# A decoder layer on one core: the routed-token table two steps behind its one-hot rows, gates scaled earlier, semaphores cleared on five engines

## The chip, the cores and the metric

The kernel runs on one core of one Trainium2 chip. A core has five engines that run their own instruction streams and meet only through semaphores: PE (matrix multiply), DVE (VectorE, elementwise work and reductions), ACT (ScalarE, activation functions and copies), POOL (GpSimd) and SP (SyncE, which here issues most of the DMAs). The metric is the device time of one execution, in microseconds (us); lower is better.

## The reference

The input `x` is 4 sequences of 512 tokens with 512 features, in float32. Three residual blocks follow one another, each on a layer-normalised input:

```
x = x + self_attention(layernorm(x))     # 16 heads of 32, rotary, causal, a window of 128 keys
x = x + cross_attention(layernorm(x), ctx)   # 32 heads of 16, RMS-normed q and k, softmax over 512 keys
x = x + moe(layernorm(x))                # 64 experts, 8 per token, at most 256 tokens per expert
```

The last block matters here. A router gives each token 64 logits; the softmax of its 8 largest, scaled to sum to one, are its gates. Tokens are numbered within each expert in order of appearance, those beyond 256 are dropped, and each expert runs `down(silu(gate(x)) * up(x))` on its own tokens. The results are added to the tokens' rows, weighted by the gates.

## The kernel before, in words

Three phases follow one another: `self_attention` (`sa`), `cross_attention` (`xa`) and `experts` (`ex`). Each holds its semaphores and buffers in a `Phase`, and the phases are separated by barriers of all engines. When a phase's block ends, `Phase.clear` opens a further block in which SP clears the phase's semaphores one by one (line 69), and a barrier ends that block too. This happens for six groups of semaphores: `sw` (10), `sa` (47), `xw` (8), `xa` (85), `ex` and `ew` (33 together).

The cross-attention phase is a list of steps written out by hand (`WALK`). Every engine's program is a loop over the same steps `w`, and functions such as `hot_step` or `rt_step` say in which step a piece of work stands. A batch of the attention takes 32 steps (`STEPS`), so the four batches are steps 0 to 127. In step `w`:

- PE computes the scores of step `w` (line 1420, two banks of `xa_ring`) and then the product with the values for step `w - 1` (line 1432); ACT computes the exponentials of step `w` in between (line 1038).
- Every fourth step (`w` = 1 modulo 4) PE transposes a finished group of heads (`turn_out`, line 1440). Before that DVE copies it out of the accumulator (`take_values`, line 1289, one step earlier); after it DVE divides by the sums and adds to the residual (`take_out`, lines 1205 to 1211).
- Beside this run the projections of the next batch and the routing of the batch before: `turn_route` (PE, 1378), its split into a high and a low part (ACT 1056, DVE 1199), the logits (`project_route`, PE, lines 75 to 77), `take_logits` (DVE 1217, 1219), then the choice of 8 experts, the positions, and the gates.

Engines take their instructions in the order written, so an instruction that waits holds all that stands behind it on its engine.

The routing ends in a table: for each expert and place, which token stands there. It is made for 16 tiles of 128 tokens, numbered `n`. For each tile DVE writes 8 pairs of 128x128 one-hot matrices in f16 (`slots`, lines 1269 and 1271) and PE adds their products into one PSUM bank (`add_to_table`, line 1407). The one-hot matrices have two buffers, used in turn:

```
if n >= 2:
    dve.wait_ge(s_tab, n - 1)       # slots(n): the table matmuls of tile n-2 are done
pe.wait_ge(s_hot, n + 1)            # add_to_table(n): the one-hot rows of tile n are written
```

Both sides of tile `n` stand in the step `hot_step(n)`. For the tiles of the first three batches, n = 0 to 11, these are the steps 98, 100, ... 112 and 116, 118, 120, 122, inside the attention of the last batch. The four tiles of the last batch can only come after the attention, and all stand in step 138, behind that batch's own routing.

At the end of the phase, DVE scales the last batch's gates (`scale_gates`, lines 1256 and 1258) after these four tiles, SP stores them (`store_gates`, line 916) and then issues the weight loads of expert 3 (`load_weights`, lines 1491 to 1497); those of experts 1 and 2 were issued in step 131. DVE turns the finished table into token numbers (`take_table`, lines 1277 to 1281). Then SP waits for its stores, and the barrier of the phase follows.

Of the kernel before, what the change touches and what calls it, by code (L numbers as in the profile page):

```python
# [16 lines left out]
B, S, D = 4, 512, 512  # L17
T = S // P
NT = B * T
# [23 lines left out]
class Phase:  # L43
# [20 lines left out]
    def clear(self):  # L64
        with self.nc.Block() as block:
            @block.sync
            def _(sp):
                for s in self.sems:
                    sp.sem_clear(s)


def product(pe, out, hi_l, lo_l, hi_r, lo_r, chunks, part=None, stop=True):
# [542 lines left out]
def cross_attention(nc, consts, ident, stage, shared, w_w, weights_of, context, w_router, x1, x2, xn3, token, target):  # L615
# [12 lines left out]
    with ExitStack() as ctx:  # L628
# [181 lines left out]
            return pos_step(b) + 1  # L810

        def hot_step(n):
            return STEPS * (B - 1) + 2 * (n + 1 + n // (2 * T)) if n < NT - T else pos_step(B - 1) + 1

        WALK = range(begin(0, 0) - 2, STEPS * B + 13)
        TILES = [(n, j) for n in range(B) for j in range(KQ)]
        ROUTED = [(b, t) for b in range(B) for t in range(T)]

# [69 lines left out]
        @block.sync  # L888
        def _(sp):
            def load_x(n, t):  # L890
                if n >= 2:
                    sp.wait_ge(st_x[t], 16 * (n - 1))
                    sp.wait_ge(s_xr, (n - 2) * T + t + 1)
                sp.dma_start(xs[:, n % 2, t], x1[n * T + t]).then_inc(ld_x[n % 2][t], 16)

            def load_context(n, t):
                before = (n, t - 2) if t >= 2 else (n - 1, t + 2)
                if before[0] >= 0:
                    sp.wait_ge(s_b0, USE["x", *before] + 1)
                sp.dma_start(cx[:, t % 2], context[n * T + t]).then_inc(ld_c[t], 16)  # L900

            def store_turned(n, j):
                sp.wait_ge(s_free, USE["kn", n, j] + 1)
                for part in range(2):
                    sp.dma_start(turned[n % 2, j // T, part, :, j % T * P:(j % T + 1) * P].rearrange("(c p) t -> p c t", p=P),
                                 hl[:, part].bitcast(F32)).then_inc(st_h, 16)

            def load_weights(experts):
                sp.wait_ge(s_pv, STEPS * B)
                for e in experts:  # L910
                    weights_of.load_gate_up(sp, e, e)
                    weights_of.load_down(sp, e, e)

            def store_gates(b):
                sp.wait_ge(s_gt, b + 1)
                sp.dma_start(xn3[b * T:(b + 1) * T, :, D:XW].rearrange("n p e -> p n e"), gates).then_inc(st_g, 16)

            def load_turned(n, q, side):
                sp.wait_ge(st_h, 32 * (n * KQ + T * (side + 1)))
                if n > 0:  # L920
                    for i in range(2):
                        sp.wait_ge(s_sc[i], STEPS * (n - 1) + 2 * T * (q + 1))
                rows = turned[n % 2, side].rearrange("a (pair i d) t -> a i d pair t", i=2, d=D2)
                for r, part in enumerate(((0, 1, 0), (0, 0, 1))[side]):
                    for i in range(2):
                        at_row = i * W2 + r * D2
                        sp.dma_start((kT, qT)[side][at_row:at_row + D2, 4 * q:4 * q + 4, :].bitcast(F32),
                                     rows[part, i, :, 4 * q:4 * q + 4, :]).then_inc(ld_h[q], 16)

            def store_x2(b, t):  # L930
                sp.wait_ge(s_x2, (b + 1) * G)
                sp.dma_start(x2[b * T + t], xs[:, b % 2, t]).then_inc(st_x[t], 16)

            def store_normal(b, t):
                sp.wait_ge(s_xr, b * T + t + 1)
                sp.dma_start(xn3[b * T + t, :, 0:D], xn[:, route_slot(t)]).then_inc(st_n[t], 16)

            for n in range(2):
                for t in range(T):
                    load_x(n, t)  # L940
            for w in WALK:
                for n, t in at(lambda n, t: x_step(n - 1, T - 1) + 2, w, [(n, t) for n in range(1, B) for t in range(2)]):
                    load_context(n, t)
                for n, t in at(lambda n, t: x_step(n, t - 2), w, [(n, t) for n in range(B) for t in range(2, T)]):
                    load_context(n, t)
                for n, j in at(kn_step, w, TILES):
                    store_turned(n, j)
                    if n == 0 and T <= j < KQ - 1:
                        load_turned(0, j - T, 0)
                if w == kn_step(0, KQ - 1):  # L950
                    for q in range(3):
                        load_turned(0, q, 1)
                for n in range(1, B):
                    if w == kn_step(n, T - 1) + 1:
                        load_turned(n, 0, 0)
                        load_turned(n, 1, 0)
                    if w == kn_step(n, KQ - 1):
                        for q, side in ((0, 1), (1, 1), (2, 0), (2, 1)):
                            load_turned(n, q, side)
                for n in range(B):  # L960
                    if w == STEPS * n:
                        for side in range(2):
                            load_turned(n, 3, side)
                if w > STEPS and w % STEPS == 2:
                    for t in range(T):
                        store_x2(w // STEPS - 1, t)
                if w == STEPS * B:
                    load_weights(range(1))
                for r in at(rn_step, w, ROUTED):
                    store_normal(*r)  # L970
                if w == rn_step(B - 1, T - 1):
                    load_weights(range(1, 3))
                for b in range(B):
                    if w == gate_step(b):
                        store_gates(b)
                for n, t in at(lambda n, t: rn_step(n - 2, t), w, [(n, t) for n in range(2, B) for t in range(T)]):
                    load_x(n, t)
            load_weights(range(3, weights_of.AHEAD))
            for t in range(T):
                sp.wait_ge(st_x[t], 16 * B)  # L980
                sp.wait_ge(st_n[t], 16 * B)
            sp.wait_ge(st_g, 16 * B)
# [119 lines left out]
        def _(dve):  # L1102
# [188 lines left out]
            for w in WALK:  # L1291
# [25 lines left out]
                for b in range(B):  # L1317
                    if w == sel_step(b):
                        choose(b)
                for n in range(NT):  # L1320
                    if w == hot_step(n):
                        slots(n)
                for b in range(B):
                    if w == gate_step(b):
                        scale_gates(b)
            take_table()
            dve.wait_ge(s_x2, B * G)

# [1 line left out]
        def _(pe):  # L1330
# [112 lines left out]
            for w in WALK:  # L1443
# [19 lines left out]
                    if 0 <= step < (C if j < T else 2):  # L1463
                        project(n, j, step)
                for n in range(NT):
                    if w == hot_step(n):
                        add_to_table(n)


# [393 lines left out]
```

## Time and profile before

| | us |
|---|---|
| median of 3 runs (lowest to highest) | 1760.61 (1759.91 to 1761.31) |
| the profiled execution | 1763.67 |
| its span, first to last instruction | 1761.9 |
| PE busy in it | 1443.3 (82%) |
| DVE busy, ACT busy | 1052.7, 980.6 |
| mean granted clock of PE | 0.914 of full |

The span is divided roughly so: the self-attention phase ends at 520, the exponentials of the cross-attention run from 633 to 1165, the routing of the last batch from there to 1208, and the first work of the experts begins at 1216. Busy time is the time in which an engine had an instruction in flight. "Idle before, releaser" in a row gives how long the engine had been idle and which instruction ended that. A queue row (`SPq`, `DVEq`) is an instruction of an engine's instruction stream that does no data work, such as a barrier (`DRAIN`, `EVENT_SEMAPHORE`) or a DMA issue.

### The profile page before, as it was taken

The page shows a single profiled execution, that of the slowest core. Times are in us where ns is not written, and L with a number is a line of the kernel's source. Part 1 is how long each engine was busy: PE and PEld are TensorE (multiplying, and loading weights), DVE is VectorE, ACT ScalarE, POOL GpSimd, SP SyncE. Part 2 cuts the span into 40 slices and gives each one's busy share as a digit, 9 for nine tenths or more (in the row PEclk, how much of TensorE's full clock was granted, in tenths as well). Part 3 has the DMA queues.
Part 4 walks back from the last instruction along what each step waited for, and adds up shares of the span by engine and source line. Part 5 has one row for each costly group of instructions (what it writes and reads, how often), then busy time and mean ns, then how long its engine had stood idle before and what let it go on. Part 6 is the DMA issues. An engine that isn't in the chain of part 4 may idle for free. (4 is left out here: it accounts for less than half of the span.)

```text
span 1761.9 us, 28899 instructions
## 1 busy us (share of the span) xinstructions
PE 1443.3 (82%) x9667; PEld 1066.1 (61%) x9667; DVE 1052.7 (60%) x2102; ACT 980.6 (56%) x1982; POOL 771.0 (44%) x494
## 2 busy tenths in 40 slices
PE   3988898989966578988988856672999999999990
PEld 2777776777744444444444323242899999999880
DVE  4667576666636524344444453445888888888880
ACT  3555454545532246755755733431777787777770
POOL 2444343443432024434434400001577777777762
PEclk9999899989987989999999976775999999999995
DMA  8000000000012581691681670033799999999986
GB/s 308 1 25 13 13 25 25 13 13 25 7 36 72 116 147 56 116 188 37 111 180 35 110 123 1 4 128 120 212 300 291 301 301 296 296 299 288 294 169 120
DMA packets 133108, 229.82 MB, mean 130 GB/s; under 512 B 17865, under 2 KB 51145, under 8 KB 132496
## 3 DMA queue, kind: packets, MB, share of 16 engines
q1 hardware_dynamic: 103184, 154.98, 32.3%
q0 software_dynamic: 29248, 72.53, 18.6%
q8 instruction: 63, 1.03, 0.2%
q10 hardware_dynamic: 576, 0.98, 0.2%
q14 instruction: 37, 0.30, 0.1%
HBM read 163.78 MB, written 71.83 MB: 134 GB/s over the span
## 5 line engine op out<-in xcount | busy, mean ns | idle before, releaser
L1038 ACT ACTIVATE shared<-xa_ring 128x1024 f32<-128x1024 f32 x256 | 247.2, 1029 | 142.9 <-PE xa_ring L1420 142.6
L1000 POOL TENSOR_TENSOR shared<-shared,xa_half 128x32 f32<-128x32 f32 x24 | 130.3, 5429 | 244.7 <-DVE shared L1159 244.7
L282 POOL TENSOR_TENSOR sa_prob<-sa_prob,sa_rinv 128x1024 f32<-128x1024 f32 x64 | 121.3, 1896 | 247.5 <-DVE sa_rinv L445 247.5
L1587 POOL DMA_INDIRECT ex_xg<-xn,token x128 | 169.3, 1322 | 86.5 <-issue 56.8
L340 ACT ACTIVATE sa_prob<-sa_sc_ps,sa_nmax 128x256 f32<-128x256 f32 x256 | 118.0, 473 | 113.4 <-DVE sa_nmax L432 113.4
L75 PE MATMUL ex_ba<-ex_xh,ex_wh 128*128 128x256 f32 x512 | 150.8, 295 | 5.8 <-DVE ex_xl L1701 3.7
L1432 PE MATMUL xa_out<-shared 128*17 128x512 f32 x1024 | 148.4, 654 | 0.6 <-ACT shared L1038 0.4
L76 PE MATMUL ex_ba<-ex_xl,ex_wh 128*128 128x256 f32 x512 | 146.1, 285 | 0.0
L77 PE MATMUL ex_ba<-ex_xh,ex_wl 128*128 128x256 f32 x512 | 146.0, 285 | 0.0
L1688 DVE TENSOR_TENSOR ex_wl<-shared,ex_wh 128x1024 fp32r<-128x1024 f32 (+1 forms) x128 | 116.9, 955 | 41.0 <-ACT ex_wh L1631 40.9
L432 DVE TENSOR_REDUCE sa_nmax<-sa_sc_ps 128x2 f32<-128x512 f32 x128 | 83.1, 687 | 67.6 <-PE sa_sc_ps L577 67.6
L1420 PE MATMUL xa_ring<-xa_qT,xa_kT 64*128 64x512 f32 x512 | 107.0, 489 | 12.6 <-DMA xa_qT<-turned 6.3
L1598 POOL DMA_INDIRECT out_dram<-ex_y,target x64 | 104.5, 1632 | 23.1 <-issue 23.1
L1631 ACT ACTIVATE ex_wh<-shared 128x1024 fp32r<-128x1024 f32 (+1 forms) x128 | 100.2, 832 | 25.4 <-PEq L1538 25.4
L1598 POOL DMA_INDIRECT odd_sum<-ex_y,target x64 | 104.3, 1629 | 22.5 <-issue 19.2
L75 PEld LDWEIGHTS ex_ba<-ex_xh,ex_wh 128*128 128x128 f32 x512 | 98.9, 193 | 22.4 <-issue 22.4
L76 PEld LDWEIGHTS ex_ba<-ex_xl,ex_wh 128*128 128x128 f32 x512 | 99.3, 194 | 0.0
L77 PEld LDWEIGHTS ex_ba<-ex_xh,ex_wl 128*128 128x128 f32 x512 | 99.3, 194 | 0.0
L573 PE MATMUL sa_sc_ps<-sa_mask,sa_identb 128*128 128x512 bf16 x128 | 53.7, 419 | 43.8 <-DVE sa_kT L412 30.9
L1701 DVE TENSOR_TENSOR ex_xl<-ex_bx,ex_xh 128x512 fp32r<-128x512 f32 x128 | 82.6, 686 | 9.5 <-issue 7.0
L1420 PEld LDWEIGHTS xa_ring<-xa_qT,xa_kT 64*128 64x128 f32 x512 | 43.5, 201 | 70.5 <-issue 37.7
L75 PE MATMUL sa_pr_ps<-sa_wh,sa_xh 128*128 128x512 f32 x192 | 84.6, 441 | 1.5 <-DVE sa_xl L389 1.5
(235 smaller groups left out, 4024.4 us busy)
## 6 DMA issues: line engine op xcount, KB each, us to landing
shared<-in_L_ffn_gate_proj_dram SPq DMA_DIRECT2D x64, 384.0 KB
shared<-in_L_ffn_up_proj_dram SPq DMA_DIRECT2D x64, 384.0 KB
turned<-stage SPq DMA_DIRECT2D x64, 256.0 KB, 2.8
shared<-in_L_ffn_down_proj_dram SPq DMA_DIRECT2D x64, 256.0 KB
xa_kT<-turned SPq DMA_DIRECT2D x96, 128.0 KB, 7.3
xa_qT<-turned SPq DMA_DIRECT2D x96, 128.0 KB, 9.0
shared<-in_L_ffn_down_proj_dram SPq DMA_DIRECT2D x64, 128.0 KB
sa_x<-in_x_dram SPq DMA_DIRECT2D x16, 256.0 KB, 2.8
```

What stands on the lines that cost most here:

```text
L75: pe.matmul(out, hi_l(c), hi_r(c), start=(c == 0), stop=False)
L76: pe.matmul(out, hi_l(c), lo_r(c), start=False, stop=False)
L77: last = pe.matmul(out, lo_l(c), hi_r(c), start=False, stop=(stop and c == chunks - 1))
L282: pool.tensor_tensor(prob[:, 4 * g:4 * g + 4, :], prob[:, 4 * g:4 * g + 4, :], rinv[:, 4 * g:4 * g + 4].unsqueeze(2).to_broadcast([P, 4, 2 ...
L340: act.activation(prob[:, h, :], sc_ps[p][:, i, :], ACT.Exp, bias=nmax[:, h:h + 1], accum_out=rsum[:, h:h + 1]).then_inc(s_ex[p], 1)
L1000: pool.tensor_tensor(power[:, i], ms[:, i], half[:], ALU.pow).then_inc(s_pw, 1)
L1038: act.activation(prob[:, w % 2, 2 * i:2 * i + 2, :], ring[i][:], ACT.Exp, scale=D2 ** -0.5).then_inc(s_ex[i], 1)
L1420: last = pe.matmul(ring[u][:, i, :], kT[half, pair, kt * P:(kt + 1) * P], qT[half, pair, :], start=True, stop=True)
L1432: last = pe.matmul(out_ps[32 * i:32 * i + D2 + 1, :], v[:, b % 2, kt, 4 * g + i, :], prob[:, w % 2, i, :], start=(kt == 0), stop=(kt == T ...
L1587: pool.indirect_dma_start(out=xg[:, e % RING, j, :], out_offset=None, in_=xn3, in_offset=bass.IndirectOffsetOnAxis(token[:, at:at + 1], 0))\
L1598: pool.indirect_dma_start(out=odd_sum if e % 2 else out, out_offset=bass.IndirectOffsetOnAxis(target[:, at:at + 1], 0), in_=y[:, e % RING, ...
L1688: dve.tensor_tensor(lo, src, hi.bitcast(F32), ALU.subtract).then_inc(s_wl, 1)
```

## The change

Four edits are made. The table matmuls of tile `n` stand two steps behind its one-hot rows on PE; the last four tiles' rows are spread over steps 138 and 139, so their matmuls stand in steps 140 and 141, and `WALK` is a step longer. In a step, `scale_gates` stands ahead of `slots`. The loads of expert 3's weights stand with those of experts 1 and 2 in step 131, ahead of the last gates' store. Each semaphore group is cleared on all five engines, a fifth on each.

```diff
@@ class Phase, def clear
             @block.sync
             def _(sp):
-                for s in self.sems:
+                for s in self.sems[0::5]:
                     sp.sem_clear(s)
+
+            @block.tensor
+            def _(pe):
+                for s in self.sems[1::5]:
+                    pe.sem_clear(s)
...
(the same on vector [2::5], scalar [3::5] and gpsimd [4::5])
@@ cross_attention
         def hot_step(n):
-            return STEPS * (B - 1) + 2 * (n + 1 + n // (2 * T)) if n < NT - T else pos_step(B - 1) + 1
+            return STEPS * (B - 1) + 2 * (n + 1 + n // (2 * T)) if n < NT - T else pos_step(B - 1) + 1 + n % T // 2
-        WALK = range(begin(0, 0) - 2, STEPS * B + 13)
+        WALK = range(begin(0, 0) - 2, STEPS * B + 14)
@@ SP
                 if w == rn_step(B - 1, T - 1):
-                    load_weights(range(1, 3))
+                    load_weights(range(1, weights_of.AHEAD))
...
-            load_weights(range(3, weights_of.AHEAD))
             for t in range(T):
                 sp.wait_ge(st_x[t], 16 * B)
@@ DVE
+                for b in range(B):
+                    if w == gate_step(b):
+                        scale_gates(b)
                 for n in range(NT):
                     if w == hot_step(n):
                         slots(n)
-                for b in range(B):
-                    if w == gate_step(b):
-                        scale_gates(b)
@@ PE
                 for n in range(NT):
-                    if w == hot_step(n):
+                    if w == hot_step(n) + 2:
                         add_to_table(n)
```

## Rows read from the trace of the kernel before

**Rows 1.** The page: busy us, share of the span and instructions of each engine.
```profile
PE 1443.3 (82%) x9667; PEld 1066.1 (61%) x9667; DVE 1052.7 (60%) x2102; ACT 980.6 (56%) x1982; POOL 771.0 (44%) x494
```

**Rows 2.** Waits from 1017 to 1156: who waited for whom, us, times, longest.
```profile
ACT shared L1038 <- PE xa_ring L1420: 80.6, 23, 6.7
...
PE xa_pr L1407 <- DVE stage L1271: 49.4, 12, 5.7
```

**Rows 3.** Timeline, steps 99 to 101: start us, us, engine, line, operation [idle before].
```profile
1026.07 1.94 ACT L1038 ACTIVATE shared<-xa_ring 128x1024 f32<-128x1024 f32 x2 [6.70 <-PE xa_ring L1420]
...
1029.06 1.94 ACT L1038 ACTIVATE shared<-xa_ring 128x1024 f32<-128x1024 f32 x2 [1.05 <-PE xa_ring L1420]
...
1030.45 0.66 PE L1378 MATMUL xa_b<-ident,xa_xn 128*128 128x128 f32 x4
...
1033.03 1.38 DVE L1269 TENSOR_SCALAR stage<-xa_from,xa_row 128x128 f16<-128x128 f16 x8
1034.33 1.86 DVE L1271 TENSOR_SCALAR stage<-xa_from,xa_column,xa_token 128x128 f16<-128x128 f16 x8
...
1036.25 1.04 PE L1407 MATMUL xa_pr<-stage 128*128 128x128 f16 x8 [5.14 <-DVE stage L1271]
...
1038.05 1.94 ACT L1038 ACTIVATE shared<-xa_ring 128x1024 f32<-128x1024 f32 x2 [6.31 <-PE xa_ring L1420]
```

**Rows 4.** Timeline: the exponentials of steps 98, 123 with 124, and 126 with 127.
```profile
1017.43 1.94 ACT L1038 ACTIVATE shared<-xa_ring 128x1024 f32<-128x1024 f32 x2 [1.08 <-PE xa_ring L1420]
...
1155.02 3.77 ACT L1038 ACTIVATE shared<-xa_ring 128x1024 f32<-128x1024 f32 x4 [3.03 <-PE xa_ring L1420]
...
1161.51 3.77 ACT L1038 ACTIVATE shared<-xa_ring 128x1024 f32<-128x1024 f32 x4 [0.61 <-PE xa_ring L1420]
```

**Rows 5.** Windows: us, busy of PE, PEld, DVE, ACT, POOL, PEclk, DMA share, GB/s.
```profile
1017.43:1161.51 144.08, 90.93 (x531) 36.59 (x529) 63.66 (x268) 58.30 (x73) 2.60 (x6) 0.75 0.19 35
896.00:1016.00 120.00, 102.37 (x599) 50.33 (x599) 48.26 (x116) 71.76 (x101) 47.87 (x20) 0.93 0.51 103
1155.02:1163.40 8.38, 7.64 (x52) 2.20 (x50) 1.80 (x4) 7.60 (x9) 0.00 (x0) 1.00 0.01 2
1190.00:1206.00 16.00, 4.01 (x29) 2.83 (x29) 14.78 (x75) 1.04 (x7) 0.00 (x0) 0.50 0.01 2
```

**Rows 6.** Timeline: normalising for routing; a logits product at full clock; table matmuls; the gates' exponentials.
```profile
1024.13 0.73 DVE L1140 TENSOR_SCALAR xa_xn<-stage,xa_mv,xa_rstd 128x512 f32<-128x512 f32 x1
...
1051.77 0.30 PE L75 MATMUL xa_b<-xa_rh,xa_route_h 128*128 128x64 f32 x1
...
1053.34 0.23 DVE L1217 COPY xa_logits<-xa_b 128x64 f32<-128x64 f32 x1 [0.73 <-PE xa_b L77]
...
1117.26 0.30 ACT L1075 ACTIVATE xa_ex<-xa_top,xa_negative 128x8 f32<-128x8 f32 x1
...
1119.35 3.74 ACT L1038 ACTIVATE shared<-xa_ring 128x1024 f32<-128x1024 f32 x4
...
1136.76 0.62 PE L1407 MATMUL xa_pr<-stage 128*128 128x128 f16 x8 [2.71 <-DVE stage L1271]
```

**Rows 7.** Timeline of the phase's end: scaling of the gates, the last weight load's issue.
```profile
1206.11 0.43 DVE L1258 TENSOR_TENSOR xa_xn<-xa_xn,xa_total 128x256 f32<-128x256 f32 x1
...
1208.49 0.47 SPq L1497 DMA_DIRECT2D shared<-in_L_ffn_down_proj_dram  x1
```

**Rows 8.** Line 628, the phase's barrier: ns min/median/max, first and last start us.
```profile
L628 DVEq DRAIN  x1: 17/17/17, 1208.2 to 1208.2; - x1
...
L628 SPq DRAIN  x1: 7/7/7, 1209.5 to 1209.5; - x1
```

**Rows 9.** Line 69, the clears: the whole span, then 1209 to 1216 alone.
```profile
L69 SPq EVENT_SEMAPHORE_RANGE_CLEAR  x183: 25/30/49, 23.6 to 1761.6; - x183
...
L69 SPq EVENT_SEMAPHORE_RANGE_CLEAR  x85: 25/30/49, 1209.7 to 1215.0; - x85
```

**Rows 10.** Line 65, the clearing block's barrier: the semaphore instruction of PE.
```profile
L65 PEldq EVENT_SEMAPHORE  x1: 51/51/51, 1215.2 to 1215.2; - x1
```

More of the change, by code:

```diff
@@ L67, in _ @@
             def _(sp):
-                for s in self.sems:
+                for s in self.sems[0::5]:
                     sp.sem_clear(s)
+            @block.tensor
+            def _(pe):
+                for s in self.sems[1::5]:
+                    pe.sem_clear(s)
+            @block.vector
+            def _(dve):
+                for s in self.sems[2::5]:
+                    dve.sem_clear(s)
+            @block.scalar
+            def _(act):
+                for s in self.sems[3::5]:
+                    act.sem_clear(s)
+            @block.gpsimd
+            def _(pool):
+                for s in self.sems[4::5]:
+                    pool.sem_clear(s)
 def product(pe, out, hi_l, lo_l, hi_r, lo_r, chunks, part=None, stop=True):
```

## The prediction, made before the changed kernel was run

> **What bounds the kernel now.** I read the page first: PE is busy for 82% of the span [rows 1], so the other 18% are where to look. The experts' part is back to back PE work that no edit touches; the change bears on the last batch of the cross-attention (from step 98), on the phase's end, and on the blocks that clear semaphores. So next I took the waits of the last batch. PE waited 12 times, 49.4 us in all, for the last one-hot row of a tile, and ACT, which does nothing late by itself, waited 80.6 us for PE's scores [rows 2]. The timeline of steps 99 to 101 shows how: PE ends its own work of step 100 with a transpose at 1030.45 + 0.66 us; DVE only starts the tile's one-hot rows at 1033.03 and ends at 1036.2; PE's table matmuls start at 1036.25 after 5.14 us of idleness, and the next exponentials come at 1038.05, 9.0 us after the last ones. The step before, without a table, took 3.0 us [rows 3]. So DVE's 3.2 us (1.38 + 1.86) and all that DVE does ahead of them stand on the path once every other step. The windows show what this costs in clock: the stretch ran at a mean granted clock of 0.75 while DVE was busy 63.7 of 144.1 us and ACT 58.3; undisturbed steps at its end ran at 1.00 with PE busy 7.64 of 8.38 us [rows 5].
>
> **The table matmuls.** Nothing is added or removed, 96 matmuls go two steps down PE's list. I take the stretch from the exponentials of step 98 (1017.43) to those of step 126 (1161.51): 28 steps, seven groups of four, 144.1 us [rows 4, 5]. What would it take without the 12 waits?
> - Attention alone at full clock: steps 123 to 125 take 6.49 us and step 126 half of 3.77, so 8.4 a group, 58.7 for seven [rows 4].
> - 12 tables at 0.62 (the full-clock price), 7.4; four logits products at 1.57 (1051.77 to 1053.34), 6.3 [rows 6]; four transposes at 0.66, 2.6 [rows 3], and after three of the products about 0.4 each until DVE has copied the logits (0.23 plus the hand-over, an estimate), 1.2 [rows 6].
> - The positions' few matmuls, an estimate of 1.0 from the table's price; the gates on ACT, 2.1 (1117.26 to 1119.35) [rows 6]; four high-part copies on ACT, which fills 7.60 of 8.38 us by itself [rows 5]: at half an exponential (0.5) each, of which 1.3 shows.
> - A wait that appears: the first routed tile is normalised on DVE behind tile 0's one-hot rows and is ready at 1024.13 + 0.73 = 1024.9 [rows 6]; PE now comes for it at about 1017.4 + 2 x 2.1 + 0.9 = 1022.5. 2.4 us.
>
> The sum is 83.0, a gain of 61 at full clock. At the clock mix of the other batches' routing (0.93, [rows 5]), 14% of 83 us are at half clock, where a plain step takes 3.0 us instead of 1.9 [rows 3, 4]; that gives back 4.6. What else may be late: `slots(n)` now stands ahead of `take_out` of the next step, whose bank PE wants two steps later. DVE needs 3.25 + 0.7 us for both, PE takes 0.6 (table) + 2.5 + 1.9 until then, a cover of 1 us; where a routed tile's low part comes first (steps 104, 106, 110) the cover is about gone. Over seven groups DVE has 9.1 us of work in 11.9. I take off 2.5 us for that. The buffers are no new wait: `slots(n)` needs the table of tile n-2, which stands at least two steps earlier on PE. Value taken: **54 us**. Lower end 47 (the 49.4 of waits less the 2.4 that appear, and no clock back), upper end 61. It is far nearer to the upper working than to a half of it, since each term has a row.
>
> The Trainium skill ("TensorE: Matmul & The Clock Gate", Part 1) says that the array's half rate is its default and that activity releases it. By that rule alone, PE without idle waits stays at full clock and the sum is the 61 us; the trace agrees as far as it goes, with clock 0.75 where PE idled 49 us and 1.00 in the undisturbed group [rows 2, 5].
>
> **Rows of the last four tiles and the gates.** Steps 138 to 141 hold nothing else on PE, so two steps of distance change nothing there; PE still waits for DVE's last tile. DVE is the bound: 14.78 of 16 us busy [rows 5]. Scaling the gates first puts its 0.43 us [rows 7] and a small reciprocal, with the hand-over some 0.6, on that path: DVE reaches the barrier at 1208.2 + 0.6 = 1208.8 instead of 1208.2 [rows 8]. SP had been last, at 1209.5 [rows 8], since it stored the gates after the last row and then issued four weight loads up to 1208.96 [rows 7]. Both are now done four tiles (13 us) earlier. So the phase ends with DVE: 0.65 us gained, between 0 and 1. The four loads come earlier on SP, in a place where SP next waits for the gates anyway; the gates' store queues behind one more expert's weights, but the DMA engines were idle at 0.01 from 1190 to 1206 [rows 5], so it has ten us to spare. Cost nothing; if that cover were gone, the barrier would wait for it, some us. The experts' first weights were in time before and are not later now.
>
> **The clears.** SP's 85 clears run from 1209.7 to 1215.0, 63 ns each though an instruction takes 30; there are 183 [rows 9]. All stand between two barriers with every other engine idle, hence on the path: 183 x 0.06 = 11.1 us. By groups of 10, 47, 8, 85, 25 and 8, the longest share of one engine is 2 + 10 + 2 + 17 + 5 + 2 = 38 clears, 2.4 us at SP's pace. Gain **8.7**. The trace shows no clear on another engine. From one side, they cost as on SP or a bit less: 9.0. From the other, PE's barrier instruction takes 51 ns [rows 10] against the clear's 30, so 90 ns a clear: 3.4 us, gain 7.7; I put the low end at 7.
>
> **Sum.** 54 + 8.7 + 0.65 = 63.3. Against the profiled execution (span 1761.9 and 1.8 around it, 1763.7) that is 1700.4; the median of the runs is 3.1 lower, so **1697.3**.
>
> **The rivals.**
> - Clock all back: PE is fed so steadily that the 4.6 and the 2.5 us aren't lost. 61 + 9.3 = 70.4, so 1690. For it: the undisturbed steps. Against: the 2.4 us stall, and the batches before, with less idleness than now, were at 0.93. Chance 0.17.
> - Clock not back: the stretch keeps its mix, PE having small gaps in every step. 47 + 9.3 = 56.3, so 1704. Chance 0.18.
> - DVE becomes the bound: it takes over the order, and each of the 12 one-hot groups makes PE wait for the `take_out` or the low part behind it, about 1.1 us each (the length of `take_out`), 13 us from the 56: gain 43 + 9.3, so 1708. For it: the thin cover above. Against: 77% of DVE's time. Chance 0.1.
> - The change doesn't do what it says: the 49 us were hidden beside something else (a load of keys, ACT), and the stretch stays: only the 9.3 us come, 1751. Against: ACT waits 80.6 us for PE and for nothing else there [rows 2]. Chance 0.02.
> - Slower: the clears. Instructions of a kind that only SP has run so far, in new program parts on four engines, are slow to fetch or to run on one of them. Place: the six clearing blocks; it decides from (63.3 + 2.4) / 38 = 1.7 us a clear, against 63 ns now. At 2 us each: 38 x 2 = 76 us against a gain of 54.7 + 11.1, so 1771. Against: PE's 51 ns [rows 10]. Chance 0.02.
>
> **How the numbers follow.** The forecast has 0.51, at 1697, by itself 1693 to 1702. To hold 8 of 10 the range takes in half-way to each neighbour and both clock cases: 1688 to 1709. A change within 0.2% (3.5 us) is what a measurement here can't tell from none. Faster by more: forecast and the first four rivals, 0.97; slower 0.02; within it 0.01.
>
> **What would show it.** Right: in the stretch no wait of PE's table matmuls for DVE longer than a few tenths of a us; 28 steps in 83 to 97 us; clock there 0.9 or more; a first wait of PE for the normalised tile of 1 to 3 us; the clears of the big group within 1.1 to 1.6 us; the phase's last barrier set by DVE. Wrong: PE waiting at the logits or transposes for DVE's `take_out` or copies (DVE the bound), clock below 0.85 with no waits (the second rival), or a clear pitch above 0.1 us on any engine. Should the stretch shrink as worked out and the total not, something in the experts has moved, for which I have no row.

## The result and the profile after

The changed kernel takes 1686.6 us (median of 4 runs, 1675.9 to 1692.4) against 1760.3 before (4 runs, 1757.4 to 1761.3): a ratio of 0.958 [0.953, 0.963]. The forecast was 1697, with a range of 1688 to 1709; the kernel is 1.4 us faster than the range's lower end. The profiled executions took 1692.4 and 1763.7 us, 71.3 us apart where 63.3 were forecast.

The page of the changed kernel answers to [rows 1]: PE does the same 9667 matmuls and is busy for 84% of a shorter span. The second line is from the page's list of costliest groups: ACT waits 76.4 us for scores in the whole kernel; the same line of the kernel before had 142.6.

```profile
PE 1424.7 (84%) x9667; PEld 1062.2 (63%) x9667; DVE 1050.2 (62%) x2102; ACT 978.9 (58%) x1982; POOL 772.4 (46%) x494
...
L1057 ACT ACTIVATE shared<-xa_ring 128x1024 f32<-128x1024 f32 x256 | 247.1, 1030 | 76.5 <-PE xa_ring L1439 76.4
```

The waits of PE for other engines in the changed kernel, from the exponentials of step 98 to those of step 126, answer to [rows 2]. Columns: us in total, times, longest.

```profile
PE xa_ring L1439 <- ACT shared L1057: 2.7, 6, 1.0
PE xa_b L1397 <- DVE xa_xn L1159: 2.2, 1, 2.2
PE xa_b L1397 <- DVE xa_logits L1236: 1.2, 3, 0.4
PE xa_b L95 <- DVE xa_scaled L1226: 0.8, 1, 0.8
...
PEld xa_pr L1426 <- DVE stage L1290: 6.0, 7, 0.9
```

The wait of the table matmuls for the one-hot rows, 49.4 us in 12 pieces, is gone. What is left was foreseen: one wait of 2.2 us for the normalised tile, three of 0.4 for the logits, and one of 0.8 for `take_out`. The last line is of the weight loads (`PEld`), which run beside the matmuls: for 7 of the 12 tables they still waited for a row, up to 0.9 us, while PE was busy with its own work of the step. So the rows are ready in time, but not by much.

The windows of the changed kernel answer to [rows 5]: the same 28 steps, a stretch of the batch before, and the phase's end up to the clears. Columns as in [rows 5].

```profile
1017.41:1096.67 79.26, 72.25 (x531) 30.58 (x529) 62.89 (x268) 58.08 (x73) 2.60 (x6) 0.94 0.32 61
896.00:1016.00 120.00, 101.52 (x599) 49.96 (x599) 48.08 (x116) 71.37 (x101) 47.85 (x20) 0.93 0.47 100
1096.67:1144.00 47.33, 23.68 (x135) 18.46 (x133) 29.64 (x120) 8.36 (x20) 1.22 (x2) 0.58 0.44 147
```

The stretch starts within 0.02 us of where it did and takes 79.3 us instead of 144.1: 64.8 less, out of the 71.3. The same 531 matmuls now fill 72.25 us instead of 90.93, because the granted clock in the stretch is 0.94 where it was 0.75. That is near the 0.93 of the stretch ahead of it, which the change doesn't touch.

The timeline around step 100 answers to [rows 3]. Columns: start us, us, engine, line, operation [idle before].

```profile
1026.71 1.94 ACT L1057 ACTIVATE shared<-xa_ring 128x1024 f32<-128x1024 f32 x2 [0.53 <-PE xa_ring L1439]
...
1027.48 1.39 DVE L1288 TENSOR_SCALAR stage<-xa_from,xa_row 128x128 f16<-128x128 f16 x8
...
1028.78 1.87 DVE L1290 TENSOR_SCALAR stage<-xa_from,xa_column,xa_token 128x128 f16<-128x128 f16 x8
...
1030.25 1.94 ACT L1057 ACTIVATE shared<-xa_ring 128x1024 f32<-128x1024 f32 x2 [1.60 <-PE xa_ring L1439]
...
1031.35 0.62 PE L1426 MATMUL xa_pr<-stage 128*128 128x128 f16 x8
...
1032.44 1.94 ACT L1057 ACTIVATE shared<-xa_ring 128x1024 f32<-128x1024 f32 x2 [0.25 <-PE xa_ring L1439]
```

DVE's one-hot rows take as long as before (1.39 + 1.87), but they end at 1030.6, and the table matmuls that stand in the list at 1031.35 find them ready; the next exponentials come 2.2 us after the last ones.

The clears answer to [rows 9]. The first line is SP's share of the group of 85 at the end of the cross-attention, the others PE's and DVE's, from the instructions of the lines that hold them in the changed kernel. Columns: ns min/median/max, first and last start us.

```profile
L69 SPq EVENT_SEMAPHORE_RANGE_CLEAR  x17: 25/25/35, 1144.0 to 1145.0; - x17
...
L74 PEldq EVENT_SEMAPHORE_RANGE_CLEAR  x17: 56/56/56, 1144.1 to 1146.0; - x17
...
L79 DVEq EVENT_SEMAPHORE_RANGE_CLEAR  x17: 54/54/54, 1144.1 to 1145.4; - x17
```

SP starts a clear every 57 ns, DVE every 83, PE every 117 (ACT 67 and POOL 64 by the same reading). PE's 17 clears last 1.9 us and set the block's end. In the line below, the phase's last barrier, DVE is the last to come (PE's drain started 2 us earlier), as in the forecast.

```profile
L648 DVEq DRAIN  x1: 17/17/17, 1143.8 to 1143.8; - x1
```

Where the 71.3 us come from: 64.8 from the stretch; 0.85 from the rest of the phase (48.18 to 47.33); 3.2 between the big group's first clear and the experts' first instruction (6.70 to 3.51); 0.8 behind the experts (2.34 to 1.50); 1.6 from the experts' part (543.15 to 541.53), which no edit touches. At step 98 the two executions are level, though the clearing blocks before it are 1.5 us shorter in the changed one; the same code around them took that much longer there.

### The profile page after: what moved, and what is told of

The parts are those of the page before. It is cut to its first block and busy times, and to the rows that moved or that the text cites. A ratio compares the mean times of both kernels' runs of the same rounds, so it can differ in the third digit from the quotient of the medians.

```text
span 1690.5 us, 28899 instructions
## 1 busy us (share of the span) xinstructions
PE 1424.7 (84%) x9667; PEld 1062.2 (63%) x9667; DVE 1050.2 (62%) x2102; ACT 978.9 (58%) x1982; POOL 772.4 (46%) x494
## 5 line engine op out<-in xcount | busy, mean ns | idle before, releaser
L1057 ACT ACTIVATE shared<-xa_ring 128x1024 f32<-128x1024 f32 x256 | 247.1, 1030 | 76.5 <-PE xa_ring L1439 76.4
L1606 POOL DMA_INDIRECT ex_xg<-xn,token x128 | 173.3, 1354 | 83.0 <-issue 60.5
L97 PE MATMUL ex_ba<-ex_xh,ex_wl 128*128 128x256 f32 x512 | 146.1, 285 | 0.0
L1451 PE MATMUL xa_out<-shared 128*17 128x512 f32 x1024 | 140.5, 622 | 0.5 <-ACT shared L1057 0.4
L1439 PE MATMUL xa_ring<-xa_qT,xa_kT 64*128 64x512 f32 x512 | 103.4, 473 | 14.0 <-DMA xa_qT<-turned 7.5
L1665 ACT ACTIVATE ex_sg<-ex_ba 128x256 f32<-128x256 f32 x64 | 24.5, 383 | 108.6 <-PE ex_bb L97 108.6
```

The costliest lines, as they stand in the source:

```text
L97: last = pe.matmul(out, lo_l(c), hi_r(c), start=False, stop=(stop and c == chunks - 1))
L1057: act.activation(prob[:, w % 2, 2 * i:2 * i + 2, :], ring[i][:], ACT.Exp, scale=D2 ** -0.5).then_inc(s_ex[i], 1)
L1439: last = pe.matmul(ring[u][:, i, :], kT[half, pair, kt * P:(kt + 1) * P], qT[half, pair, :], start=True, stop=True)
L1451: last = pe.matmul(out_ps[32 * i:32 * i + D2 + 1, :], v[:, b % 2, kt, 4 * g + i, :], prob[:, w % 2, i, :], start=(kt == 0), stop=(kt == T ...
L1606: pool.indirect_dma_start(out=xg[:, e % RING, j, :], out_offset=None, in_=xn3, in_offset=bass.IndirectOffsetOnAxis(token[:, at:at + 1], 0))\
```

## Experiments

All runs give "stretch" from the exponentials of step 98 to those of step 126, and "tail" from there to the first clear. Totals of single executions scatter by some 5 us, since the self-attention ended at any time from 507.9 to 520.6 us with the same code; so parts are compared by these stretches, and totals by the ratios of runs on one chip.

**1. Each part alone, and the changed kernel again.**

```
table_only    + hot_step of the last four tiles: + n % T // 2; WALK one longer
              - if w == hot_step(n):          (add_to_table on PE)
              + if w == hot_step(n) + 2:
clears_only   - for s in self.sems: sp.sem_clear(s)
              + for s in self.sems[i::5]: engine_i.sem_clear(s)   on five engines
tail_only     + scale_gates ahead of slots; load_weights(range(1, AHEAD)) in step 131
```

> The changed kernel once more, beside its three parts. Both theories: 1675 to 1692 as its four runs had it, median near 1687; stretch from the exponentials of step 98 to those of step 126 79 to 85 us in its profile.

> Only the table matmuls two steps behind their one-hot rows (with the spread of the last four tiles). Theory A (nearly all of the extra 10 us over the forecast lies in this stretch: the table matmuls hide half beside the exponentials, and neither the clock nor DVE takes back what was set aside for them): 65 us faster than before, about 1695, stretch 79 to 81 us. Rival B (the forecast's 54 us was right for this part and the rest came from the end of the phase and the experts' start): 54 us faster, about 1706.

> Only the clears on five engines. From PE's pace of 117 ns a clear in the changed kernel's trace, 38 clears in sequence cost 4.4 us: theory A 6 us faster than before (5 to 7), 1754. Rival B (clears and what they start earlier give 8.7 or more): 1751 or less.

> Only the gates' scaling ahead of the last rows and expert 3's weights loaded with those of experts 1 and 2. Theory A: the phase's barrier 0.6 to 0.9 us earlier, total within 1 us of that, 1759.5. Rival B (the earlier weight loads free the DMA engines for the experts' first gathers): 2.5 us or more faster.

Against the kernel before on the same chip (1758.75, 23 runs): the changed kernel 0.9575 [0.9541, 0.9610]; the tables alone 0.9624 [0.9586, 0.9661], so 66 us; the clears alone 0.9963 [0.9941, 0.9985], 6.5 us; the tail's edits 0.9988 [0.9967, 1.0009], 2.1 us and not told from none. The stretches were 78.5, 78.3, 143.8 and 146.1 us. The window of the stretch with the tables alone:

```profile
1014.56:1092.82 78.26, 71.13 (x531) 31.34 (x529) 62.92 (x268) 58.08 (x72) 2.60 (x6) 0.96 0.40 68
```

The table edit alone gives the whole gain of the stretch, the clears' blocks come out at 3.51 and 1.50 us wherever the edit is in, and the totals of the parts add up (66 + 6.5 + 2.1 against 74.7 us). The tail's shares don't: it is 47.37 us with the tail's edits alone, but also 47.50 with the table edit alone, and 47.33 with both, against 48.18 before. Spreading the last rows over two steps has the gates scaled ahead of the last two tiles, and SP reaches the barrier 5 us ahead of DVE without the tail's edits; so either edit gains about 0.7 to 0.8 us there and the second one next to nothing.

**2. Is it the wait or the clock?** The kernel before, with its waits, but ahead of each of the 12 waits PE runs ten matmuls of 512 columns whose result nobody reads.

```
  def add_to_table(n):
+     ...   (for n = 0, waits until that bank is free)
+     if n < NT - T:
+         for _ in range(10): pe.matmul(pr[:, 0], ones, ones..., start=True, stop=True)
      pe.wait_ge(s_hot, n + 1)
```

> The kernel before with 10 matmuls of 128x512 bf16 (into a bank that nothing reads) put into each of PE's 12 waits for one-hot rows: the waits stay, PE is not idle in them. Theory A (18 of the 65 us that the stretch lost are the clock, as PE's busy time for the same instructions fell from 90.9 to 72.0 us): granted clock 0.9 or more and stretch 126 to 134 us instead of 144 to 146. Rival B (the clock follows the attention's own small gaps, not these waits): clock 0.8 or less, stretch 142 us or more.

1744.8 us in one execution against 1755.5 beside it. The stretch in this kernel, then PE's wait for the rows that is left behind the ten matmuls:

```profile
1014.20:1146.34 132.14, 107.31 (x651) 43.73 (x649) 63.76 (x268) 58.07 (x73) 2.60 (x6) 0.90 0.23 40
```

```profile
PE xa_pr L1413 <- DVE stage L1271: 20.8, 12, 3.4
```

With 120 matmuls more, the stretch is 12 us shorter, and the clock 0.90 instead of 0.75, as theory A had it; each of the 12 tables still waits for its rows. So the idle waits cost clock as well as their own length: of the 64.8 us at least 12 can be had by clock alone. The rest, 53 at most, needs the order.

**3. One step behind instead of two.**

```
- if w == hot_step(n) + 2:
+ if w == hot_step(n) + 1:
```

> The changed kernel with the table matmuls one step behind their rows instead of two. Theory A (one step of 1.8 to 2.2 us covers less than the 3.2 us of rows, so PE waits 1 to 1.5 us in each of 12 places, and little of the clock is lost): stretch 90 to 98 us. Rival B (any distance will do, since the wait only has to leave the step in which the rows are written): 79 to 82 us.

1713.5 us, the stretch 101.9. PE's waits in it, then its window:

```profile
PE xa_pr L1426 <- DVE stage L1290: 17.0, 10, 3.4
```

```profile
1017.32:1119.18 101.86, 79.58 (x531) 32.79 (x529) 63.10 (x268) 57.66 (x73) 2.59 (x6) 0.87 0.26 49
```

Against the changed kernel 22.6 us are lost. 17.0 of them are waits; the other 5.6 go with the lower clock (0.87). The second step is needed; with one, PE waits for the rows at 10 of the 12 tiles, 1.7 us on average. That is more than either theory allowed: theory A had the waits at 1 to 1.5 us and little loss of clock.

**4. What do the table matmuls cost when nothing waits?** First one table matmul of eight for each of the 12 tiles (the table is then incomplete), then every table matmul twice, the second into a bank that nobody reads.

```
light_tables   - for k in range(TOPK):
               + for k in (range(TOPK) if n >= NT - T else 1 of 8):
double_tables  + for k in range(TOPK): pe.matmul(pr[:, 0, 0:P], row_at[:, i, k], token_at[:, i, k], ...)
               ...   (for n = 0, waits until that bank is free)
```

> The changed kernel with 1 of 8 table matmuls for each of tiles 0 to 11 (the table is then incomplete); 83 or 84 matmuls fewer in the stretch from step 98 to step 126, everything else as it was. Theory A (a table group costs PE only 0.3 us of the path, the rest hides while ACT computes exponentials): stretch 3 to 4 us shorter than the 78.5 to 79.3 measured. Rival B (the full 0.62 of the forecast each): 6 to 7 us shorter.

> The changed kernel with the table matmuls of tiles 0 to 11 done a second time into a bank that nothing reads: 96 more matmuls on PE, and no other work. Theory A (a group costs 0.3 to 0.4 us of the path, since PE and ACT share the step's time and half of it hides): stretch 3.5 to 5 us longer than 78.3 to 79.3. Rival B (0.62 each, as the forecast had it): 7.4 us longer or more.

The window of the stretch with one eighth of the matmuls:

```profile
1012.21:1091.46 79.25, 70.36 (x448) 27.23 (x445) 62.87 (x268) 57.62 (x72) 2.60 (x6) 0.91 0.35 64
```

and with twice as many:

```profile
1011.57:1092.22 80.65, 73.39 (x627) 34.74 (x625) 62.93 (x268) 57.97 (x73) 2.60 (x6) 1.00 0.29 63
```

83 matmuls fewer gave no time at all, and 96 more cost 1.4 us: by the whole stretch neither theory holds in either run. But the clock differs, 0.91 and 1.00 against 0.94, and its lower level falls on different steps. From step 111 to step 114 the kernel with one eighth (first line) ran mostly at half clock and lost 4.1 us against the changed kernel (second line):

```profile
1052.28:1063.99 11.71, 11.71 (x55) 4.91 (x53) 8.03 (x37) 5.81 (x7) 0.00 (x0) 0.57 0.01 1
1059.47:1067.11 7.64, 7.64 (x62) 3.73 (x60) 7.18 (x35) 5.82 (x7) 0.00 (x0) 1.00 0.01 2
```

So the stretch as a whole can't price a table; steps at full clock can. In the changed kernel the four steps 119 to 122, with two tables, run from 1080.92 to 1089.92 (the first row holds steps 119 and 120):

```profile
1080.92 3.77 ACT L1057 ACTIVATE shared<-xa_ring 128x1024 f32<-128x1024 f32 x4 [0.26 <-PE xa_ring L1439]
1085.42 1.94 ACT L1057 ACTIVATE shared<-xa_ring 128x1024 f32<-128x1024 f32 x2 [0.73 <-PE xa_ring L1439]
1087.65 1.94 ACT L1057 ACTIVATE shared<-xa_ring 128x1024 f32<-128x1024 f32 x2 [0.29 <-PE xa_ring L1439]
1089.92 3.77 ACT L1057 ACTIVATE shared<-xa_ring 128x1024 f32<-128x1024 f32 x4 [0.33 <-PE xa_ring L1439]
```

The windows of this group in the changed kernel, with one eighth of the table matmuls, and with twice as many:

```profile
1080.92:1089.92 9.00, 8.71 (x70) 3.26 (x68) 8.01 (x39) 7.65 (x8) 0.00 (x0) 1.00 0.00 0
1076.52:1084.84 8.32, 8.01 (x54) 2.50 (x54) 8.11 (x37) 7.53 (x8) 0.00 (x0) 1.00 0.01 2
1075.12:1085.02 9.90, 9.58 (x86) 4.11 (x84) 8.85 (x43) 7.65 (x9) 0.00 (x0) 1.00 0.01 2
```

All three at full clock: seven of a table's eight matmuls cost 0.34 us, and doubling a table costs 0.45. Against the 8.38 us of a group without tables [rows 5], 0.31 us a table. This is theory A's price, and half of the 0.62 that the forecast took. PE's rows in the doubled kernel show part of the reason:

```profile
1078.53 0.62 PE L1430 MATMUL xa_pr<-stage 128*128 128x128 f16 x8
1078.99 0.61 PE L1432 MATMUL xa_pr<-stage 128*128 128x128 f16 x8
```

Each eight are busy for 0.62 us, but the second eight start 0.46 us behind the first: the end of a row's busy time overlaps what comes next. That the rest, from 0.46 down to some 0.33, fills idle time that the group had anyway is an inference.

**5. How near is DVE to being the bound?** Eight, then two, one-hot operations more per tile, into a buffer of their own, ahead of the real ones.

```
  def slots(n):
+     if 0 < n < NT - T:
+         ...   (two waits of DVE)
+         for k in range(TOPK):       (heavy_two: range(2))
+             dve.tensor_scalar(spare[:, k], from1[:], row[:, n, k:k + 1], None, ALU.is_equal)
```

> The changed kernel with 8 more one-hot operations (1.4 us of DVE, into a buffer that nothing reads) ahead of the rows of tiles 1 to 11, 15 us in all. Theory A (DVE has cover in most steps, so the 2.5 us set aside for it were not needed): less than half of it shows, the stretch grows by 2 to 7 us. Rival B (DVE's cover is used up, as the forecast feared): it grows by 12 us or more.

> The changed kernel with 2 more one-hot operations on DVE (0.35 us, into a buffer that nothing reads) ahead of the rows of tiles 1 to 11, 3.9 us in all. Theory A (small cover is left in nearly every place, so that nothing of DVE's order shows in the changed kernel and the 2.5 us set aside were not spent): stretch up to 1 us longer. Rival B (the cover is used up): 3 us longer or more.

With eight more the stretch is 90.6 us. Its window, then PE's waits for DVE in it:

```profile
1017.68:1108.31 90.63, 74.22 (x531) 30.89 (x529) 76.90 (x356) 58.09 (x72) 2.60 (x6) 0.92 0.29 55
```

```profile
PE xa_pr L1432 <- DVE stage L1296: 6.2, 7, 1.4
...
PE xa_b L1403 <- DVE xa_logits L1237: 2.5, 3, 1.6
PE xa_b L1403 <- DVE xa_xn L1160: 2.2, 1, 2.2
PE xa_b L95 <- DVE xa_scaled L1227: 1.9, 2, 1.1
```

DVE is busy 14.0 us more (76.90 to 62.89) and the stretch is 11.4 longer, 8.6 of it in PE's waits for DVE (12.8 to 4.2). With two more it is 82.0:

```profile
1009.39:1091.41 82.02, 73.57 (x531) 32.07 (x529) 66.36 (x290) 58.21 (x72) 2.60 (x6) 0.92 0.34 63
```

DVE is busy 3.5 us more and the stretch is 2.8 us longer; PE's waits for DVE grew by 1.0 us. Step by step the 2.8 us divide: the 22 steps that ran at full clock in both kernels grew by 1.2 us, and steps 106 and 107, at a clock of 0.67 instead of 0.80, by 1.6. Whether DVE's work made the clock fall there isn't shown; the same two steps took 7.3 us in the doubled kernel of experiment 4, where the clock was full, and 8.5 to 8.7 in the changed one. So of two more operations a tile about a third comes out at full clock, near theory A's bound of 1 us, and four fifths with the clock; of eight more, four fifths, near theory B. A little cover is left: some 0.2 us of DVE's time a tile, an estimate from what didn't come out (2.3 of 3.5 us, 2.6 of 14.0). Beyond it what DVE gets in addition shows in full, so DVE's work in this stretch is still worth removing.

**6. The one wait that appeared.** The one-hot rows of tiles 0 and 1 in steps 94 and 96, where the timeline shows DVE with room, so that the first routed tile is normalised earlier.

```
  def hot_step(n):
+     if n < 2: return STEPS * (B - 1) - 2 + 2 * n
```

> The changed kernel with the rows of tiles 0 and 1 in steps 94 and 96 instead of 98 and 100, where DVE sits idle. Theory A (the routed tile's normalising is late only because tile 0's rows stand ahead of it): the wait of 2.2 us in step 100 goes and no other comes in its place; from the exponentials of step 98 to those of step 126 76 to 77.5 us, and nothing lost in steps 94 to 97. Rival B (as in the run before, another wait takes its place): 78.5 us or more.

The stretch took 75.5 us, 3.8 less than in the changed kernel, and the wait for the normalised tile fell from 2.2 to 0.4:

```profile
PE xa_b L1399 <- DVE xa_xn L1161: 0.4, 1, 0.4
```

The wait is 1.8 of the 3.8 us. One of the 12 tables has moved ahead of the stretch with its rows (523 matmuls in it instead of 531), some 0.3 us, and the clock was 0.95 instead of 0.94; against the changed kernel's other execution, at 0.96, the difference is 3.0. In steps 94 to 97 the two early tiles cost next to nothing at full clock: 10.5 us with the tables alone (experiment 1), 10.7 in the first run of experiment 9. The total of this single execution (1688.0) can't show 3.8 us.

**7. The clears by the engines' own pace.**

```
+ cost = {"sync": 57, "gpsimd": 64, "scalar": 67, "vector": 83, "tensor": 117}
+ for s in self.sems: give s to the engine with the least load + cost
```

> The changed kernel with each engine's share of the clears set by its measured pace (SP 57 ns, POOL 64, ACT 67, DVE 83, PE 117) instead of a fifth each. Theory A (PE's pace alone sets the end of each clearing block): the group of 85 takes 1.3 us instead of 2.1, from its first clear to the experts' first instruction 2.7 us instead of 3.51; over all groups 1.6 us less. Rival B (the barrier and its hand-overs set it): under 0.3 us less.

The shares in the big group, which all last 1.2 us now:

```profile
L76 SPq EVENT_SEMAPHORE_RANGE_CLEAR  x22: 25/28/35, 1141.1 to 1142.3; - x22
...
L76 DVEq EVENT_SEMAPHORE_RANGE_CLEAR  x15: 54/54/54, 1141.1 to 1142.3; - x15
L76 PEldq EVENT_SEMAPHORE_RANGE_CLEAR  x10: 56/56/56, 1141.2 to 1142.3; - x10
```

From first clear to first instruction of the experts 2.71 us instead of 3.51, at the end 1.15 instead of 1.50. PE's pace was the limit.

**8. Three trials on the tail.** Filler matmuls ahead of PE's long wait before the last routing; all one-hot rows of the last tile on POOL (with the weighted clears, and tile 0's rows a step later); both together, with filler around the experts' first gather.

```
fill_tail    + keep_busy(4) in step 128; keep_busy(20) in step 132   (the filler of experiment 2)
split_pool   + for k in range(TOPK): pool.tensor_scalar(...)         (tile 15's 16 operations)
all_in       + split_pool, fill_tail, 40 and 12 f32 fillers around the experts' first turn(0)
```

> The changed kernel with 4 and then 20 matmuls of 128x512 bf16 into a bank that nothing reads, in PE's idle time between the last attention step and the last batch's routing. Theory A (the clock is what idle time costs, here as in the stretch: the four logits products run at half clock behind that idle time): tail from the exponentials of step 126 to the first clear 41 to 43 us instead of 47.3 (or 44.8, as in one run), total 4 us faster. Rival B (the chain through DVE and ACT sets the tail): under 1 us, or slower if the filler outlasts the idle time.

> The changed kernel with weighted clears, tile 0's rows a step later (behind the first routed tile's normalising), and the one-hot rows of the last tile, 15, written by POOL into buffers of their own beside DVE's three. Theory A: stretch 1.5 to 2 us shorter (the wait for the normalised tile goes), tail 2.5 to 3.1 us shorter (DVE 9.3 instead of 12.4 us), 6 us faster in all. Rival B (POOL is slow at it, over 0.6 us an operation, or slows DVE): tail the same or longer.

> split_pool with the tail's filler, and filler matmuls on PE while it waits for the experts' first gather. Theory A: the sum of the two and 1 to 2.5 us at the experts' start, 11 us faster than the changed kernel, about 1673. Rival B: no more than split_pool.

Against the kernel before on that chip: 0.9595 [0.9558, 0.9633], 0.9589 [0.9563, 0.9615] and 0.9613 [0.9589, 0.9636], none told from the changed kernel. With the filler the tail is 47.24 us. PE in that kernel:

```profile
1100.46 4.48 PE L1464 MATMUL xa_pr<-xa_ones 128*128 128x512 bf16 x20
1107.02 3.13 PE L1397 MATMUL xa_ring<-ident,xa_xn 128*128 128x128 f32 x16 [2.07 <-DVE xa_xn L1159]
1109.80 0.40 PE L95 MATMUL xa_ring<-xa_rh,xa_xh 128*128 128x64 f32 x1
```

The filler ended at 1104.9 and left an idle wait of 2.07 us. The transposes behind it still began at full clock, which was granted up to 1108.57; in the changed kernel it fell 7.9 us into the tail, here 14.8. But it fell all the same, and the logits take 0.40 us each, the price of the lower clock. The transposes took 3.13 us instead of 3.67 and began 0.5 us later, so the tail gained 0.1. Covering most of one wait moved the fall of the clock and didn't prevent it; why it fell under the transposes isn't shown. On POOL the operations took 0.66 and 0.88 us each, and DVE's beside them 0.28 and 0.34:

```profile
L1298 DVE TENSOR_SCALAR stage<-xa_from,xa_column,xa_token 128x128 f16<-128x128 f16 x24 | 6.2, 344 | 0.0
...
L1038 POOL TENSOR_SCALAR stage<-xa_from,xa_column,xa_token 128x128 f16<-128x128 f16 x8 | 7.0, 880 | 0.0
...
L1036 POOL TENSOR_SCALAR stage<-xa_from,xa_row 128x128 f16<-128x128 f16 x8 | 5.2, 658 | 20.2 <-DVE xa_row L1279 20.2
```

so the last tile came 0.6 us earlier at most (tail 46.8). In the third kernel the 40 f32 fillers ran as one stretch of 79 matmul instructions (each filler is two) and outlasted the wait that they were to cover; the first gathered tile's transposes came 11.8 us after the experts' first instruction, against 7.7 in the second kernel.

```profile
1138.41 11.78 PE L1812 MATMUL ex_by<-ident 128*128 128x128 f32 x79 [4.07 <-PEq L1576]
```

**9. What pointed to a gain, together.** Tiles 0 and 1 early, clears by pace, five of eight pairs of the last tile on POOL, and the 15 starting increments of the experts' counters on SP, POOL and ACT.

```
+ early_rows, clears_weighted
+ ON_POOL = 5                                   (pairs of tile 15)
- for c in counters: sp.sem_inc(c, START)
+ for c in counters[i::3]: engine_i.sem_inc(c, START)    i = SP, POOL, ACT
```

> early_rows with the weighted clears, the experts' 15 counter increments shared by SP, POOL and ACT, and 5 of the 8 one-hot pairs of tile 15 written by POOL (0.66 and 0.88 us an operation against DVE's 0.25 and 0.31). Theory A: stretch 2 us, tail 1 us, clears and increments 2.2 us less, 5 us faster than the changed kernel, about 1680. Rival B (the parts hide behind one another): 2 us or less.

> The last version again. Theory A (its parts add up, as its profile's stretches say: 4.5 us in the stretch, 1.1 at the clears, 0 to 1.6 in the tail): 5 to 7 us faster than the changed kernel on the same chip, stretch 74 to 76 us. Rival B: within 2 us of it.

> The changed kernel again, beside the last version. Both theories: ratio to before 0.955 to 0.960, stretch 78 to 80 us.

The first time 1681.35 (6 runs), 0.9557 [0.9522, 0.9591], not told from the changed kernel. Beside the changed kernel on one chip: 1673.8 (5 runs, 1669.4 to 1676.8), 0.9518 [0.9496, 0.9541], against 1681.5 (5 runs, 1680.3 to 1683.5), 0.9569 [0.9550, 0.9588]. The slowest of its runs is 3.5 us below the fastest of the changed kernel. The medians are 7.7 us apart, the profiled executions 6.5. In these the last version gains 5.7 in the stretch (79.29 to 73.61, at a clock of 1.00 against 0.94), 4.0 in the tail, 1.1 between clears and experts (3.51 to 2.45), 0.3 at the end and 0.6 in the experts' part, and loses 5.3 ahead of the stretch. Of the tail's 4.0 about 2.5 aren't the edit's: the changed kernel's tail itself took 47.3 or 44.8, and 44.8 in each of the four executions of this document (experiments 1, 3, 4, 5) in which the clock came back to full for a while some 17 us into it, as it did here.

## Why the prediction was right and where it was wrong

- **The waits go, PE is the bound.** Right: no wait of the table matmuls for DVE in the stretch, and the rival in which DVE takes over (1708) didn't occur; the wait for the normalised tile was put at 2.4 us and is 2.2, those for the logits at 0.4 each and are 0.4. The stretch lies in neither the 83 to 97 us named as its sign nor the 47 to 61 us of gain: it took 79.3.
- **The step that failed is the size of the stretch's term, 54 us against 64.8 measured.** The forecast's 90.1 us were 83.0 at full clock, 4.6 for the clock and 2.5 for DVE. Taking for each step the fastest of three executions (the changed kernel twice, the tables alone) gives 75.7 us as the full-clock time, an estimate from their timelines. Experiment 9 bears it out: at a clock of 1.00 its stretch took 73.6, with 1.9 us less of the wait for the normalised tile and one table less. So 7.3 us too much stood in the working, 1.0 in the clock (3.6 instead of 4.6), and 2.5 for DVE's lateness, whose one visible wait, 0.8 us, lies within the 75.7.
- **Within the 83.0 us** the tables were one half of the fault. I took the matmuls' busy time, 0.62 us each. In groups of steps at full clock a table costs 0.31 to 0.35, and 0.45 where it is a second one (experiment 4), so 12 tables were 3.3 to 3.7 us too dear. The other 3.6 to 4.0, by subtraction, are in the logits, transposes, copies and the gates, whose durations I summed in the same way; no run takes one of these alone, so how they divide isn't shown. Both are one fault: durations were added to a group although they overlap their neighbours and the group holds idle time on both engines. The "upper end" was thus no bound. A group of attention steps was put at 8.38 us; from start to start the trace has 8.31 (1155.02 to 1163.33), another 0.5 us over seven groups and part of those 3.6 to 4.0.
- **The clock.** Right in kind: 0.75 went to 0.94, where 0.93 had been assumed (the lower level that is left lies on steps 100 and 101, 106 and 107, 116 and 117), and experiment 2 shows that the clock alone, with the waits in place, is worth 12 us. That PE's 18.7 us of busy time (90.93 to 72.25) would fall was in the sum.
- **The tail.** 0.85 us against 0.65, with DVE last at the barrier. Right in size. The working gave it to the gates' scaling and the weight loads, and took the spread of the last tiles to change nothing; experiment 1 shows that the spread alone brings 0.7 of it.
- **The clears.** 8.7 forecast, 5.6 found in the profiles (0.2, 1.2, 0.1, 3.2 and 0.8 at the blocks), 6.5 +- 3.9 by the runs of that edit alone. The low end took 90 ns a clear from PE's 51-ns instruction; the pace on PE is 117, twice the instruction's 56 rather than 1.8 times. At 117 ns the 38 clears of the longest shares come to 4.4 us, a gain of 6.6; the clears in fact took 11.0 us before and 5.3 after, since a block of a few clears is longer than its clears at that pace (0.30 us for two).
- **The experts** moved by 1.6 us in the profiled pair without an edit to them. In all kernels their part took from 538.8 to 543.6 us, in no order that an edit explains; it isn't resolved.

So the gain was 10.8 us above the forecast in the stretch, 0.2 above in the tail, 3.1 below in the clears, and 1.6 above by the experts; 1.5 us of the clears, at the early blocks, don't show in this pair, which is level at step 98. That gives 63.3 + 10.8 + 0.2 - 3.1 + 1.6 - 1.5 = 71.3. The rival "clock all back" (1690) came nearest in time, but that is luck: the clock wasn't all back.

## What to carry to other kernels

When a wait goes and two engines both have slack in a step, price the remaining operations by what a group of steps grows by where the trace has the group with and without them, not by their busy time; an "upper end" of summed durations bounds nothing. A consumer that waits for another engine every second step pays for its idle time twice, in length and in granted clock, and moving its work down its list until the producer is always done (here by two steps, one was not enough) gave nearly all of both back. Split serial housekeeping by each engine's own pace, not by equal counts.

## What the runs showed of the hardware

- In the group of 85, a semaphore clear is issued every 57 ns on SP, 64 on POOL, 67 on ACT, 83 on DVE and 117 on PE (119 on average over all 17).
- A stretch with 448 matmuls, one with 531 and one with 627 took 79.25, 79.26 and 80.65 us, at mean granted clocks of 0.91, 0.94 and 1.00, in one execution each. The difference of the clock lies in single steps: 7.6 us at full clock for steps 111 to 113, 11.7 at 0.57.
- Eight 128x128 matmuls in f16 at full clock are busy for 0.62 us, and the next eight start 0.46 us behind them.
- A comparison into 128x128 f16 took 247 ns on DVE and 658 on POOL, with a multiply 306 and 880; DVE's own slowed by about 12% while POOL ran them (280 and 344 ns).
- Filler on PE that ended 2 us ahead of the next work kept the full clock up to 1.5 us into that work; then it fell to half with PE at work.
- The same code of the self-attention ended between 507.9 and 520.6 us; its mean clock was 0.94 in the execution that ended at 520.6 and 0.97 in one that ended at 508.9.
